# One ring of three PSUM banks for projections and transposes, instead of two banks and one

## What is computed

```
x = x + attention(layernorm(x))          # 32 query heads on 16 key/value heads, head size 64
x = x + ffn(layernorm(x))                # 256 -> 64 -> 1024 -> gelu -> 64 -> 256
attention(z): q, k, v = split(z @ W_qkv);  scores = q k^T / 8 + alibi bias, causal
              out = softmax(scores) @ v;   return out @ W_out
ffn(z):       gelu((z @ U1) @ V1 + b1) @ U2 @ V2 + b2
```

## Time and profile before

| | |
|---|---|
| median of 3 runs | 3042.26 us (3040.5 to 3043.39) |
| the profiled execution | 3041.37 us |
| its span | 3039.6 us, so 1.8 us lie around the span |
| granted TensorE clock, mean | 0.993 |

### The profile page before, as it was taken

How to read it: one execution, slowest core, us unless ns; L and a number is a source line. 1 busy time by engine, 2 the same in 40 slices (tenths; PEclk the granted TensorE clock), 3 DMA queues, 4 the chain that set the end, 5 groups by cost and what they waited for, 6 DMA issues and landing times.

```text
span 3039.6 us, 99681 instructions
## 1 busy us (share of the span) xinstructions
PE 2813.3 (93%) x32328; PEld 1966.0 (65%) x32328; DVE 2194.7 (72%) x6987; ACT 2190.9 (72%) x3892; POOL 1730.0 (57%) x1560
## 2 busy tenths in 40 slices
PE   4999999999989999999999999999899999999986
PEld 1666675766757666676666767667676666767664
DVE  6777677776767777677776777767677776777763
ACT  3767777777777777777777777777777777776783
POOL 1555565555655656555565665556555555565664
PEclk9999999999999999999999999999999999999998
DMA  5332232322223222232322323222232322323210
GB/s 169 68 72 58 63 71 46 79 58 69 62 55 77 53 72 60 56 76 49 78 58 60 73 47 79 55 72 60 56 75 50 77 59 56 73 48 82 55 35 8
DMA packets 220087, 195.25 MB, mean 64 GB/s; under 512 B 41738, under 2 KB 217866, under 8 KB 219274
## 3 DMA queue, kind: packets, MB, share of 16 engines
q1 hardware_dynamic: 219540, 188.32, 26.3%
HBM read 27.73 MB, written 8.39 MB: 12 GB/s over the span
## 4 chain that ended last, share of the span: by engine, by line
PE 31%; issue 27%; POOL 27%; ACT 5%; DVE 3%; POOLq 1%; ACTq 0%; DVEq 0%
POOL p_lo L1090 26%; PE proj L445 13%; PE scores L445 7%; PE o_acc L445 6%; PE max_scores L445 2%; PE ffn_acc L445 2%; ACT h_f L824 1%; ACT L738 1%; DVE v_lo L851 1%; ACT p_f L738 1%; ACT L824 1%; POOL h_lo L1113 1%; PE transposes L567 1%; DVE max_scores L925 1%; POOLq L327 1%
## 5 line engine op out<-in xcount | busy, mean ns | idle before, releaser
L1090 POOL TENSOR_TENSOR p_lo<-p_f,p_hi 128x512 f16<-128x512 f32 x1280 | 1476.6, 1158 | 1073.3 <-ACT p_hi L696 1070.8
L738 ACT ACTIVATE p_f<-scores 128x512 f32<-128x512 f32 x1280 | 756.4, 591 | 333.9 <-PE scores L445 211.5
L696 ACT ACTIVATE p_hi<-p_f 128x512 f16<-128x512 f32 x1280 | 802.3, 627 | 48.0 <-issue 33.7
L925 DVE CUSTOM_DVE_ANT_0 max_scores<-max_scores,causal 128x384 f32<-128x384 f32 (+3 forms) x1184 | 564.1, 508 | 274.6 <-PE max_scores L445 265.3
L445 PE MATMUL scores<-q_hi_lo,k_lo_hi 128*128 128x512 f16 (+3 forms) x2048 | 613.1, 300 | 28.4 <-issue 28.0
L445 PE MATMUL scores<-q_hi_aug,k_hi_aug 128*128 128x512 f16 (+3 forms) x2048 | 585.7, 299 | 0.0
L445 PE MATMUL o_acc<-v_hi_one,p_lo 128*128 128x65 f16 x5120 | 517.6, 194 | 13.7 <-POOL p_lo L1090 13.7
L445 PE MATMUL o_acc<-v_hi_one,p_hi 128*128 128x65 f16 x5120 | 517.9, 194 | 0.0
L445 PE MATMUL o_acc<-v_lo,p_hi 128*128 128x64 f16 x5120 | 517.7, 193 | 0.0
L445 PEld LDWEIGHTS o_acc<-v_hi_one,p_lo 128*128 128x128 f16 x5120 | 471.7, 98 | 49.7 <-issue 12.8
L445 PEld LDWEIGHTS o_acc<-v_lo,p_hi 128*128 128x128 f16 x5120 | 468.4, 98 | 19.5
(11 more groups left out here) (115 smaller groups left out, 5205.9 us busy)
## 6 DMA issues: line engine op xcount, KB each, us to landing
q_hi_aug<-q_pair_hi SPq DMA_DIRECT2D x512, 64.0 KB, 2.0
q_hi_lo<-q_pair_hi SPq DMA_DIRECT2D x512, 64.0 KB, 2.1
q_hi_lo<-q_pair_lo SPq DMA_DIRECT2D x512, 64.0 KB, 2.0
k_hi_aug<-k_pair_hi SPq DMA_DIRECT2D x256, 64.0 KB, 2.0
k_lo_hi<-k_pair_hi SPq DMA_DIRECT2D x256, 64.0 KB, 2.0
k_lo_hi<-k_pair_lo SPq DMA_DIRECT2D x256, 64.0 KB, 2.2
x_rows<-in_L_attn_inputs SPq DMA_DIRECT2D x17, 512.0 KB, 3.7
x_residual<-in_L_attn_inputs SPq DMA_DIRECT2D x16, 512.0 KB, 3.7
```

Of the source, the lines that this page charges most:

```text
L696: return nc.scalar.activation(out_ap, in_ap, ACT.Copy, scale=scale)
L738: nc.scalar.activation(p_f[:, k % 3, :], score_bank[k % 2][:, :], ACT.Exp).then_inc(exp_done, 1)
L925: last = nc.vector.tensor_tensor_reduce(out=bank, in0=bank, in1=causal[:, (T - 1 - qt) * P:S], scale=1.0, scalar=-3e38, op0=ALU.add, op1=A ...
L1090: nc.gpsimd.tensor_tensor(p_lo[:, slot, n, :], p_f[:, k % 3, :], p_hi[:, slot, n, :], ALU.subtract).then_inc(lo_p, 1)
```

## The change

The bank `transposes` becomes a third projection bank. The 22 transposes enter the list of uses at their places in PE's order, which makes 88, and the k-th use takes bank k mod 3. The readers take their bank from the same table. The wait ahead of each write is as before on the reader of the bank's last use; at the start of a pass a bank waits for its last use of the pass before, and, where that one belongs to the FFN, for its last use outside the FFN too. The wait between the first image's two pairs of transposes goes, since they stand in two banks.

```diff
@@ -131,10 +131,16 @@
                 uses.append(("max", s))
+            if n == out_segment(s):
+                uses.append(("o", s))
+            if (s, n) in X_PAIRS:
+                uses.append(("x", X_PAIRS[s, n]))
             if n == K_SEG and s % 2 == 1:
...
                 uses.append(("out", s))
+            if (s, n) in LN2_T_AT:
+                uses.append(("ln2", LN2_T_AT[s, n]))
             if (s, n) in FFN_PAIRS:
@@ -149,7 +155,17 @@
-PROJ = {use: k % 2 for k, use in enumerate(projection_order())}
+BANKS = 3
+PROJ = {use: k % BANKS for k, use in enumerate(projection_order())}
+
+FFN_USES = ("ln2", "p", "h", "y")
+
+
+def last_uses(b):
+
+    mine = [use for use in projection_order() if PROJ[use] == b]
+    steady = [use for use in mine if use[0] not in FFN_USES]
+    return {mine[-1], steady[-1]}
@@ -281,8 +297,7 @@
         o_bank = psum("o_acc")
-        proj_bank = [psum("proj0"), psum("proj1")]
-        t_bank = psum("transposes")
+        proj_bank = [psum(f"proj{b}") for b in range(BANKS)]
         ffn_bank = psum("ffn_acc")
@@ -454,40 +469,50 @@
+                bank = proj_bank[PROJ["x", pair]]
                 if pair == 0:
...
                         col = (c * 2 + t) * P
-                        last = nc.tensor.transpose(t_bank[:, col:col + P], xt[:, 2 * pair + t, c * P:(c + 1) * P], ident[:, :])
+                        last = nc.tensor.transpose(bank[:, col:col + P], xt[:, 2 * pair + t, c * P:(c + 1) * P], ident[:, :])
                 last.then_inc(pe_ln1, 1)
             transpose_x(0, 0)
-            pe.wait_ge(lo_ln1, 1)
             transpose_x(0, 1)
...
-                proj_free = [(acc_done, 16 * i - OUT_LAG), (acc_done, 16 * i - OUT_LAG)]
-                t_free = [(lo_ln1, 2 * (i + 1))]
-
-                def next_proj(use, semaphore, count):
-
+                def read_by(use, i):
+
+                    kind, k = use
+                    return {"max": (lo_m, i * 4 + (k - 6) // 4 + 1),
+                            "o": (lo_ot, i * KV + k - ATT - 1),
+                            "x": (lo_ln1, 2 * (i + 1) + k + 1),
+                            "k": (lo_k, i * (KV // 2) + (k + 1) // 2),
+                            "out": (acc_done, 16 * i + k - OUT_LAG + 1),
+                            "ln2": (lo_ln2, (i - 1) * 4 + k + 1),
+                            "h": (gelu_done, (i - 1) * FC + k + 1),
+                            "q": (lo_q, i * KV + k + 1),
+                            "v": (lo_v, i * 8 + k // 8 * 4 + k % 8 + 1),
+                            "p": (lo_pp, (i - 1) * 4 + k + 1),
+                            "y": (y_done, 2 * (i - 1) + k + 1 + FREE)}[kind]
+
+                def read_before(use):
+
+                    return (y_done, 2 * (i - 1) + FREE) if use[0] == "y" else read_by(use, i - 1)
+
+                proj_free = [[read_before(use) for use in sorted(last_uses(b))] for b in range(BANKS)]
+
+                def next_proj(use):
                     b = PROJ[use]
-                    read, times = proj_free[b]
-                    if times > 0:
-                        pe.wait_ge(read, at(times))
-                    proj_free[b] = (semaphore, count)
+                    for read, times in proj_free[b]:
+                        if times > 0:
+                            pe.wait_ge(read, at(times))
+                    proj_free[b] = [read_by(use, i)]
                     return proj_bank[b]
-
-                def transposes_bank(semaphore, count):
-                    read, times = t_free[0]
-                    if times > 0:
-                        pe.wait_ge(read, at(times))
-                    t_free[0] = (semaphore, count)
-                    return t_bank
@@ -561,7 +586,7 @@
                     a = i * KV + s - ATT - 2
-                    bank = transposes_bank(lo_ot, a + 1)
+                    bank = next_proj(("o", s))
                     pe.wait_ge(o_done, at(2 * (a + 1)))
@@ -659,11 +684,11 @@
                             pair = X_PAIRS[s, n]
-                            transposes_bank(lo_ln1, 2 * (i + 1) + pair + 1)
+                            next_proj(("x", pair))
                             transpose_x(i + 1, pair)
...
                             pair = (s - 1) // 2
-                            project(next_proj(("k", s), lo_k, i * (KV // 2) + pair + 1), QD + pair * P, pe_k)
+                            project(next_proj(("k", s)), QD + pair * P, pe_k)
                         if n == OUT_SEG and out_in(mode, s):
@@ -796,7 +821,7 @@
                                     act.wait_ge(pe_op, at(out_before(i, s)))
-                            copy(ot[0][:, a_slot(s) % OUT_RING, :], t_bank[:, :]).then_inc(hi_ot, 1)
+                            copy(ot[0][:, a_slot(s) % OUT_RING, :], proj("o", s)[:, :]).then_inc(hi_ot, 1)
                         if (s, n) in X_PAIRS and mode != LAST:
@@ -972,7 +997,7 @@
                             dve.wait_ge(hi_ot, at(g - ATT - 1))
-                            low(ot[1][:, a_slot(s) % OUT_RING, :], t_bank[:, :], ot[0][:, a_slot(s) % OUT_RING, :],
+                            low(ot[1][:, a_slot(s) % OUT_RING, :], proj("o", s)[:, :], ot[0][:, a_slot(s) % OUT_RING, :],
                                 1.0).then_inc(lo_ot, 1)
```

More of the change, by code:

```diff
@@ L534, in transpose_max @@
                     gr = i * 4 + (s - 6) // 4
-                    bank = next_proj(("max", s), lo_m, gr + 1)
+                    bank = next_proj(("max", s))
                     pe.wait_ge(max_done, at(4 * SEG * (gr + 1)))
@@ L578, in project_v @@
                     t, half = s % 8, s // 8
-                    bank = next_proj(("v", s), lo_v, i * 8 + half * 4 + t + 1)
+                    bank = next_proj(("v", s))
                     col = QD + KD + half * 512
@@ L587, in project_out @@
                     group, t = out_use(s)
-                    bank = next_proj(("out", s), acc_done, 16 * i + s - OUT_LAG + 1)
+                    bank = next_proj(("out", s))
                     if t == 0:
@@ L598, in transpose_x2 @@
                     u = (i - 1) * 4 + t
-                    bank = transposes_bank(lo_ln2, u + 1)
+                    bank = next_proj(("ln2", t))
                     pe.wait_ge(x2n_done, at(u + 1))
@@ L606, in ffn_p @@
                     u = (i - 1) * 4 + t
-                    bank = next_proj(("p", t), lo_pp, u + 1)
+                    bank = next_proj(("p", t))
                     pe.wait_ge(lo_ln2, at(u + 1))
@@ L615, in ffn_h @@
                     for c in (2 * pair, 2 * pair + 1):
-                        bank = next_proj(("h", c), gelu_done, (i - 1) * FC + c + 1)
+                        bank = next_proj(("h", c))
                         if c == 0:
@@ L632, in ffn_y @@
                 def ffn_y(pair):
-                    bank = next_proj(("y", pair), y_done, 2 * (i - 1) + pair + 1 + FREE)
+                    bank = next_proj(("y", pair))
                     if pair == 0:
@@ L676, in body @@
                                 pe.wait_ge(lo_ln1, at(2 * (i + 1)))
-                            project(next_proj(("q", s), lo_q, i * KV + s + 1), s * P, pe_q)
+                            project(next_proj(("q", s)), s * P, pe_q)
                         if n in (1, 3) and in_stage(mode, s, ATT + 1):
@@ L705, in high_x @@
                 copy(xnt[0][:, :, pair * 256:(pair + 1) * 256],
-                     t_bank[:, :].rearrange("p (c q) -> p c q", c=DC)).then_inc(hi_ln1, 1)
+                     proj_bank[PROJ["x", pair]][:, :].rearrange("p (c q) -> p c q", c=DC)).then_inc(hi_ln1, 1)
             high_x(0, 0)
@@ L817, in body @@
                                 act.wait_ge(pe_pp, at(u + FREE))
-                                copy(x2nt[0][:, :, :], t_bank[:, 0:D].rearrange("p (c q) -> p c q", c=DC)).then_inc(hi_ln2, 1)
+                                copy(x2nt[0][:, :, :], proj("ln2", LN2_T_AT[s, n])[:, 0:D].rearrange("p (c q) -> p c q", c=DC)).then_inc(hi_ln2, 1)
                             if (s, n) in FFN_PAIRS:
@@ L902, in low_x @@
                 cols = slice(pair * 256, (pair + 1) * 256)
-                low(xnt[1][:, :, cols], t_bank[:, :].rearrange("p (c q) -> p c q", c=DC),
+                low(xnt[1][:, :, cols], proj_bank[PROJ["x", pair]][:, :].rearrange("p (c q) -> p c q", c=DC),
                     xnt[0][:, :, cols], 1.0).then_inc(lo_ln1, 1)
@@ L1011, in body @@
                                 dve.wait_ge(hi_ln2, at(u + 1))
-                                low(x2nt[1][:, :, :], t_bank[:, 0:D].rearrange("p (c q) -> p c q", c=DC),
+                                low(x2nt[1][:, :, :], proj("ln2", LN2_T_AT[s, n])[:, 0:D].rearrange("p (c q) -> p c q", c=DC),
                                     x2nt[0][:, :, :], 1.0).then_inc(lo_ln2, 1)
```

## The result

| | before | changed |
|---|---|---|
| median of 20 runs each | 3044.20 us (3040.50 to 3049.66) | 3051.01 us (3043.37 to 3060.95) |
| the profiled execution | 3041.37 us | 3044.14 us |
| its span, its mean granted clock | 3039.6 us, 0.993 | 3042.3 us, 0.988 |

The ratio is 1.0022, with a 95% interval from 1.0014 to 1.0031: the changed kernel is slower by 0.22%, or 6.8 us. The forecast was 3029.7, and 3051.0 lies outside the range of 3014 to 3041. The three banks did remove the waits. The time came from a place that no term of the prediction covers: TensorE's granted clock.

What follows compares the result with a forecast made beforehand. PE was busy 93% of the span, but in the FFN stretch ACT was the engine that seldom waits. Start 5.4 plus MID 7.2 made 12.6 us, 3041.4 to 3028.8, plus 0.9 for the median: 3029.7; range 3014 to 3041.

Steps and rivals of the forecast that it cites:

- The start: First image's beginning: q(0) 1.9 us earlier, k(1) and the first maxima's scores 5.4 earlier; 5.4 us counted as gain.
- From there the first image runs in step with DVE: After the first maxima's scores: PE waits on DVE's maxima nearly every step, and DVE starts about 5.4 us earlier.
- MID: FFN stretch, steps 13 and 14, of 15 middle passes: PE leaves 0.48 us earlier each, 7.2 us in all.
- the lead of 0.94 at h(3): FFN stretch: h(3) starts at about 871.55 instead of 872.49, so PE leads by 0.94 us.
- the casts back to back: DVE in the FFN stretch: casts h_hi(2) and h_hi(3) ran back to back and would start 0.94 us earlier.
- ACT's first idle stretch: ACT's 0.48 us wait for PE ahead of h(2)'s table load in each pass: it goes.
- signs of being wrong: A pass shorter by over 1 us or not at all, h_hi(3) lasting 1.37, or first scores (45.62) moving under 3.
- the other 2.12 us are given back there, as a longer wait for the row maxima: FFN stretch: of 2.60 us of waits removed per pass, all but 0.48 return as longer PE waits for DVE.
- a cast that waits for POOL: Slower rival: POOL's subtraction delays h_hi(3), DVE 0.94 us later per pass, 14.1 in all; 3051.0 us, chance 0.1.
- hidden altogether: Rival in the FFN stretch: longer row-maxima waits absorb the whole lead, leaving the start; 3036.9 or 3040.4 us, chance 0.2.
- Its second: ACT's 1.00 us idle ahead of h(6)'s table load: forecast stays; rival says it goes too, 3014.7 us, chance 0.15.
- The waits for v's copies: PE's bank waits at max(10), k(11) and q(12), 27.3 us and what belongs to it: they stay, nothing counted.

Runs made afterwards that it cites:

- run 9: Changed kernel with the start's old waits put back and max(14) again waiting for h(4)'s gelu in MID passes: 3034.90 us, ratio 0.9963 to the kernel before.
- run 7: Changed kernel where in each MID pass max(14) alone waits again for the gelu of h(4): 3033.83 us, ratio 0.9967 to the kernel before.
- run 2: Changed kernel with the start's old waits put back (second pair of x's transposes, v(0), v(1)): 3057.17 us, ratio 1.0044 to the kernel before.
- run 4: Changed kernel with h(6) and h(7) issued ahead of the maxima's scores of step 14 segment 2 in MID passes: 3028.86 us, ratio 0.9952 to the kernel before.
- run 5: Changed kernel with another bank table, each use taking the bank whose last use was read first: 3007.81 us, ratio 0.9879 to the kernel before.
- run 1: Changed kernel where h(1), h(2), h(3), max(14) and out(14) wait again as before in each MID pass: 3042.17 us, ratio 0.9997 to the kernel before.
- run 3: Changed kernel with eight unused 512-column matmuls in PE's wait before step 14 segment 2's maxima scores, each MID pass: 3036.57 us, ratio 0.9979 to the kernel before.
- run 10: Changed kernel with the read-first bank table and max(14) again waiting for h(4)'s gelu in MID passes: 2997.11 us, ratio 0.9849 to the kernel before.

## Why the prediction was wrong

**The start (5.4 us forecast).** Its links held: q(0) 2.95 earlier instead of 1.9, k(1) and the DMAs behind it, the first scores 5.8 earlier instead of 5.4. What failed is "From there the first image runs in step with DVE", which carried the whole of it to the end. At the first mark 4.5 us were left in the changed kernel, by one execution of each and with 2.5 us between marks of the same program (run 9), and at the end nothing that can be told when the start alone was undone (run 9 against run 7). Where the lead went stays open. Low clock in the first image's pass plays into it: the changed kernel has three low stretches there (from 39.8, 60.3 and 74.0 us), the kernel before as much, 10.2 us in all (from 63.8 and 74.1 us), runs 2 and 9 only one. So part of what separates runs 2 and 9 from the kernel before at the first mark, 162.5 against 165.6, is the clock's and not the banks'.

**MID (7.2 us forecast, 0.48 in each pass).** Right in mechanism and nearly in size: the waits gone, the lead of 0.94 at h(3), the casts back to back, the row maxima's second wait grown to 2.05 (forecast about 2.0), ACT's first idle stretch gone (15 x 1.0 left). The interval fell from 184.05 to 183.47 us, by 0.58. None of the prediction's own signs of being wrong came: the pass is not shorter by over 1 us, no cast h_hi(3) lasts 1.37, and the first scores moved by 5.8. All its signs looked at waits, and none at the clock.

**The step that failed** is "the other 2.12 us are given back there, as a longer wait for the row maxima", priced at nothing. They were given back, 0.72 of them as the second wait for the row maxima, which grew from 1.33 to 2.05 us, and most of the rest ahead of h(3) and q(14). Behind that grown wait the granted clock fell in 9 of 15 passes. With two more low stretches at the boundary that took 19.1 us in the profiled execution, and some 6 more in the median one. Had PE's clock stayed, the time would have been near the forecast: run 7, which splits that wait and changes nothing else, is at 3033.8 with four low stretches at the boundary; by its clean intervals alone it would be 7 us less. The sum treated PE's rate as a constant. The front table's 0.993 said that it isn't, though in that trace all the low clock lies outside the MID passes, so it did not say where.

**The rivals.** The one on the slow side was a cast that waits for POOL. It did not happen: h_hi(2) and (3) took half of 0.86 us each, while h_hi(5) took 1.36 again. Its direction was right and its reason wrong, and that its price, 3051.0, is the measured time is chance. The lead was not hidden altogether, since ACT's first idle stretch went. Its second stayed until work was moved (run 4). The waits for v's copies, ahead of max(10), k(11) and q(12), stayed as said, and removing them was worth more than what the change brought: 1.9 us a pass (run 5) against 0.58. The rule of the Trainium skill that the prediction weighed (Perfetto Trace Analysis, Matmuls), to rotate independent groups through banks, left open in which order: with three banks the *order* of rotation left those waits standing, and taking the bank that is read first was worth 1.4% against the next in turn (ratios 0.9879 and 1.0022), about two thirds of it by the shorter passes.

**Shown and open.** Shown, by four edits of different kinds (runs 1, 3, 4, 7) and by run 10: the low stretches at h(6) go when the wait of 2.05 us is split or filled, and the time goes with their number. The places of the low stretches are read from one execution of each kernel; the mean clocks of the others agree. Not shown: why the clock falls in 9 passes and not in the other 6, which have the same waits (in run 2 it falls in 13 of 15), and why the boundary of passes has between none and six low stretches in different kernels. Nor did I follow the time behind the last mark, 117.3 us in run 1 against 114.9 before and 113.1 in the changed kernel.

## What to carry to other kernels

A wait that is removed ahead of another wait joins it. Before counting that as free, look at the granted clock behind the longest idle stretches of PE. If a wait would grow to the length of one behind which the clock is seen to fall now and then (here the boundary of passes, about 2 us), splitting or filling it may be worth more than removing another. Compare mean granted clocks of two kernels, and the times of passes without low clock, before explaining a difference of tenths of a per cent by dependencies. And with a ring of banks, hand out the bank that is read first, not the next in turn.

## What the runs showed of the hardware

- A wait of 2.05 us, some 7 us behind one of 1.36, was followed by 3.4 us at half the TensorE clock in 9 of 15 passes, and in 13 of 15 with the same waits in run 2; with 0.95 and 1.33 us in place of 0.22 and 2.05, it was followed by one in none of 15 (run 7). With another table of banks it was 3 of 15 (run 5), and none (run 10).
- Such a stretch cost 1.7 us where PE is the bound: a matmul of 512 columns took 0.63 us instead of 0.38.
- Eight useless matmuls in each pass (run 3) made the kernel quicker by 0.4% than without them (ratios 0.9979 and 1.0022), and so did, by 0.55%, a wait that it did not need.
- The run-to-run spread of the changed kernel (3043 to 3061 us, the same program each time) goes with the mean granted clock (0.988 to 0.983).
